# All products of a batch in halves of the rows, as one chain over three banks, from batch 1 on

## The reference

```python
def _attention(x, W_q, W_k, W_v, W_o):          # 16 heads of 16
    q, k, v = split(x @ W_q.T), split(x @ W_k.T), split(x @ W_v.T)
    attn = softmax(scale * einsum('bnqd,bnkd->bnqk', q, k))
    return merge(einsum('bnqk,bnkd->bnqd', attn, v)) @ W_o.T
...
x = x + a_alpha * _attention(_ada_rmsnorm(x, t, attn_gamma_w, attn_beta_w), W_q, W_k, W_v, W_o)
return x + f_alpha * _swiglu(_ada_rmsnorm(x, t, ffn_gamma_w, ffn_beta_w), gate_w, hidden_w, out_w, out_b)
```

## Time and profile before

| | us |
|---|---|
| median of 3 runs (lowest, highest) | 959.82 (959.23, 963.19) |
| the profiled execution, its own time | 960.88 |
| its span | 959.1 |

### The profile page before, as it was taken

One profiled execution on the slowest core, in us unless ns is written; L12 is line 12 of the kernel. 1 busy time (PEld: TensorE's weight loads), 2 busy tenths in 40 slices (PEclk: granted clock), 3 DMA queues, 4 the chain that ended last, 5 costly groups with the idle time before them and its releaser, 6 DMA issues.

```text
span 959.1 us, 18261 instructions
## 1 busy us (share of the span) xinstructions
PE 934.6 (97%) x6636; PEld 655.1 (68%) x6636; DVE 733.1 (76%) x1428; ACT 559.2 (58%) x1162; POOL 276.3 (29%) x262
## 2 busy tenths in 40 slices
PE   5999999999899999999999999999999999999998
PEld 4777777777544567767766766776677677666587
DVE  4787878999878788678778867886886788678253
ACT  5466555544566666476657646664765656476532
POOL 1256423222101033222313222231232223125142
PEclk9899999999999999999999999999999999999999
DMA  9646458434521213033022302312130222110000
GB/s 266 150 127 149 105 133 184 103 102 109 131 75 57 67 56 73 24 117 78 3 89 58 73 13 90 95 24 87 59 73 2 90 66 42 60 64 8 1 28 23
DMA packets 93754, 75.61 MB, mean 79 GB/s; under 512 B 44881, under 2 KB 79769, under 8 KB 93665
## 3 DMA queue, kind: packets, MB, share of 16 engines
q1 hardware_dynamic: 81880, 61.91, 24.5%
q10 hardware_dynamic: 11784, 12.54, 5.1%
HBM read 27.73 MB, written 12.61 MB: 42 GB/s over the span
## 4 chain that ended last, share of the span: by engine, by line
PE 86%; DVE 5%; ACT 3%; issue 2%; SPq 2%; DMA 1%; POOL 0%; ACTq 0%; DVEq 0%; POOLq 0%
PE bank L423 14%; PE bank L1083 13%; PE bank L1324 13%; PE bank L1064 9%; PE bank L1407 9%; PE raw_pair L998 5%; PE bank L1334 5%; PE bank L881 4%; PE bank L940 3%; PE bank L1146 2%; PE bank L1350 2%; PE bank L333 2%; DVE amax L486 2%; PE bank L1562 1%; PE bank L341 1%
## 5 line engine op out<-in xcount | busy, mean ns | idle before, releaser
L1072 ACT ACTIVATE probs<-bank 128x512 f32<-128x512 f32 x512 | 289.1, 599 | 201.7 <-PE bank L1064 200.5
L1008 DVE TENSOR_REDUCE rowmax<-raw_pair 128x1 f32<-128x512 f32 x488 | 325.6, 685 | 85.6 <-PE raw_pair L998 83.7
L423 PE MATMUL bank<-up_w,xs_part 128*128 128x512 f32 x768 | 193.9, 406 | 5.7 <-POOL xs_part L405 5.3
L1064 PE MATMUL bank<-q_stack,k_stack 50*128 50x512 f32 x480 | 185.9, 417 | 3.2 <-DMA q_stack<-shift_rows 1.4
L998 PE MATMUL raw_pair<-k_stack,q_stack 48*128 48x512 f32 x456 | 177.1, 413 | 0.0
L423 PEld LDWEIGHTS bank<-up_w,xs_part 128*128 128x128 f32 x768 | 144.2, 193 | 40.3 <-POOL xs_part L405 6.1
L1380 POOL TENSOR_TENSOR hid<-scratch,hid 128x512 fp32r<-128x512 f32 x64 | 84.3, 1317 | 206.1 <-ACT hid L1376 206.1
L1083 PE MATMUL bank<-probs,v_ext 128*17 128x512 f32 x1024 | 134.7, 598 | 0.6
L1064 PEld LDWEIGHTS bank<-q_stack,k_stack 50*128 50x128 f32 x480 | 82.8, 184 | 39.0 <-ACT probs L1072 25.5
L1407 PEld LDWEIGHTS bank<-out_w,hid 64*128 64x128 f32 x1152 | 87.2, 185 | 28.7 <-issue 20.4
L1407 PE MATMUL bank<-out_w,hid 64*128 64x256 f32 x1152 | 100.9, 288 | 0.2
(11 more groups left out here) (207 smaller groups left out, 1613.1 us busy)
## 6 DMA issues: line engine op xcount, KB each, us to landing
q_stack<-split SPq DMA_DIRECT2D x48, 128.0 KB, 3.4
q_stack<-hid SPq DMA_DIRECT2D x42, 128.0 KB, 2.9
k_stack<-hid SPq DMA_DIRECT2D x42, 128.0 KB, 2.9
xk<-xT SPq DMA_DIRECT2D x32, 128.0 KB, 3.0
xt<-x_tok SPq DMA_DIRECT2D x32, 128.0 KB, 2.8
x_spill<-x1t ACTq DMA_DIRECT2D x32, 128.0 KB, 2.5
xa_spill<-xa ACTq DMA_DIRECT2D x32, 128.0 KB, 2.4
x_in<-xa_spill SPq DMA_DIRECT2D x8, 512.0 KB, 5.1
```

Source lines behind the costliest of these rows:

```text
L423: last = nc.tensor.matmul(bank[j][:], xs_part[a][:, m % 2, k, :], up_w[w][:, k, col + j * W:col + (j + 1) * W], start=(i == 0), stop=(i == ...
L1008: nc.vector.reduce_max(rowmax[:, e + RAWS * half:e + RAWS * half + 1], raw_pair[:, half, :], AX.X) \
L1064: nc.tensor.matmul(score_bank[c % 2][:], k_rows[rows, slot, kt * P:(kt + 1) * P], q_rows[rows, slot, :], start=True, stop=True).then_inc(s ...
L1072: nc.scalar.activation(probs[:, (kt % 2) * J + j, :], score_bank[c % 2][:], ACT.Exp).then_inc(exp_done, 1)
```

## The change

- `plan` now gives every product of batches 1 to 7 to one chain: qk(1,0), qk(1,1) in half-step 0, then v(0), wo(0), wo(1), v(1), qk(0,0), qk(0,1) in half-steps 1 to 6, the transposes in 7, and from 8 on gate, hidden and out as before. Each is cut in lower and upper rows; the lower half of one runs beside the upper half of the one before, also across the end of a batch (the last out piece's upper half runs beside qk(1,0)'s lower half in half-step 0 of the next batch).
- The three banks of `turn_bank` are taken in turn by all products (`place`, `chain_bank`); v has counters of its own, `v_full` and `v_free`.
- Every product is complete half a step to a step later, and the consumers move: `head_act` and `head_dve` write out half-steps 0 to 7 for ScalarE and VectorE. The values of half-steps 2, 4, 6 move to the ends of 3, 4 and 6. wo waits for the high parts first and for the low ones at its eleventh matmul.
- Half-step 5 has no raw pair, 7 has two (`raws_of`). Before, that was so for no batch but the last, which left out one in 5 and ran one behind.
- The last two additions to the output of batch b - 1 move from the end of its batch into half-step 0 of the next (`out_dve`, `out_pool`), and its stores into `second_stacks_sp`, which issues ten of the twelve stack DMAs as their parts are ready; ScalarE issues the other two in half-step 3.
- In batch 7, which has no following batch, qk(0) is missing; v(1)'s upper half runs alone in half-step 5.

```diff
-        turn_bank = (psum[2], psum[3], psum[4])
+        turn_bank = (psum[3], psum[4], psum[2])
...
+        def raws_of(b, h, ffn):
+            if not ffn:
+                return [raw_at(b, h + AHEAD_FIRST)] if h < HALVES - (AHEAD_FIRST - AHEAD) else []
+            if h < RAW_PAUSE or h > RAW_PAUSE + 2:
+                numbers = [h + AHEAD]
+            else:
+                numbers = ([], [RAW_PAUSE + AHEAD], [RAW_PAUSE + AHEAD + 1, RAW_PAUSE + AHEAD + 2])[h - RAW_PAUSE]
+            return [raw_at(b, n) for n in numbers if b < B - 1 or n < RAWS * G]
...
+        def place(p):
+            if p[0] in ("gate", "hidden"):
+                return 8 + 2 * p[1] + (p[0] == "hidden")
+            if p[0] == "out":
+                return 8 + 2 * NH + p[1] // HALF
+            return {("qk", 1, 0): 0, ("qk", 1, 1): 1, ("v", 0): 2, ("wo", 0): 3, ("wo", 1): 4, ("v", 1): 5,
+                    ("qk", 0, 0): 6, ("qk", 0, 1): 7, ("xf", 1): 8, ("xf", 0): 9}[p]
+        PLACES = 8 + 2 * NH + 2
+        def chain_bank(b, p):
+            return turn_bank[(PLACES * (b - 1) + place(p)) % 3]
...
+        def chain_free_pe(pe, b, p, u, at):
+            def freed(w, count):
+                pe.wait_ge(pair_free[w], credited(pair_free[w], u + count))
+            hidden = at["hidden"]
+            if p[0] == "gate":
+                f = p[1]
+                freed(1, at["xf"][1] + 1 if f == 0 else hidden + max(f - 1, 0))
+            elif p[0] == "hidden":
+                freed(0, hidden + p[1])
+            elif p == ("out", 0, 0):
+                freed(1, hidden + NH - 1)
+            elif p == ("out", HALF, 0):
+                freed(0, hidden + NH)
+            elif p == ("qk", 1, 0):
+                freed(*((0, 0) if b == 1 else (1, -1)))
+            elif p == ("qk", 1, 1):
+                freed(1 if b == 1 else 0, 0)
+            elif p == ("v", 0):
+                freed(1, 0)
+            elif p == ("v", 1):
+                pe.wait_ge(v_free, 2 * (b - 1) + 1)
+            elif p[0] == "wo":
+                freed(p[1], at["qk1"][p[1]] + 1)
+            elif p[0] == "qk":
+                freed(p[2], at["wo"][p[2]] + 1)
...
+        def chain_lower_pe(pe, b, p, u, at):
+            c = b - 1
+            chain_free_pe(pe, b, p, u, at)
+            if p == ("gate", 0):
                 pe.wait_ge(f_in_high, c + 1)
                 pe.wait_ge(f_in_copied, c + 1)
+            elif p[0] == "qk":
+                pe.wait_ge(q_in_low, credited(q_in_low, (b if p[1] == 1 else b + 1) + 1))
+            elif p == ("wo", 0):
+                pe.wait_ge(on_high, c * GP + GP)
+            elif p[0] == "out":
+                n = OUT_PIECES.index(p[1:])
+                if n >= 2:
+                    pe.wait_ge(upper_done, (len(OUT_PIECES) - 2) * c + n - 1)
+                pe.wait_ge(prod_low, credited(prod_low, c * NH + NH // 2 * (p[2] + 1)))
...
+            steps = chain_steps(p)
+            each = len(steps) // 6
+            for i, step in enumerate(steps):
+                if p == ("gate", 0) and step[0] == 1:
+                    pe.wait_ge(f_in_low, credited(f_in_low, KD * c + (2 - step[2])))
+                elif p == ("wo", 0) and i == 10:
+                    pe.wait_ge(on_low, credited(on_low, c * GP + GP))
+                last = chain_matmul(b, p, i, step, LOWER, len(steps))
+                if i == len(steps) - 1:
                     last.then_inc(lower_done, 1)
-                yield
...
+        def chain_upper_pe(pe, b, p, u, at, lowers):
             pe.wait_ge(lower_done, lowers)
+            if p[0] == "qk":
+                w = p[2]
+                pe.wait_ge(pair_free[w], credited(pair_free[w], u + at[f"qk{p[1]}"][w]))
+            elif p[0] == "wo":
+                pe.wait_ge(pair_free[p[1]], credited(pair_free[p[1]], u + at["wo"][p[1]]))
+            elif p[0] == "v":
+                pe.wait_ge(v_free, 2 * (b - 1) + p[1])
+            elif p[0] == "out" and p[1] % HALF == HALF - 1 and p[2] == 1:
+                m = p[1] // HALF
+                pe.wait_ge(pair_free[m], credited(pair_free[m], u + at["out"]))
...
-        XF_AT, FFN_AT, OUT_AT, SPLIT_NEXT = 6, 8, 24, 25
+        XF_AT, FFN_AT, OUT_AT, SPLIT_NEXT = 7, 8, 24, 25
...
+            table[1:5] = [("v", 0)], [("wo", 0)], [("wo", 1)], [("v", 1)]
             if following:
+                table[5:7] = [("qk", 0, 0)], [("qk", 0, 1)]
...
+        VALUES_LATE = {3: 0, 4: 1, 6: 2}
+        def chain_batch_pe(pe, b, u, following, pending):
+            table, at = plan(True, following), uses(True, following)[0]
+            lowers = LOWERS * (b - 1)
+            def chain(p, middle=None):
+                nonlocal pending, lowers
+                beside_pe(None if p is None else chain_lower_pe(pe, b, p, u, at), pending, middle)
+                lowers += p is not None
+                pending = None if p is None else chain_upper_pe(pe, b, p, u, at, lowers)
+            for h in range(HALVES):
+                n = h // 2
+                def values():
+                    pb, pg = last_of(b, n // T) if n % T == 0 else (b, n // T)
+                    values_pe(pe, pb, pg, (n - 1) % T)
+                def second():
+                    excursion_pe(pe, b, h, True, (1,))
+                    if h % 2 == 0 and h > FFN_AT:
+                        values()
+                excursion_pe(pe, b, h, True, (0,))
+                if h == 0:
+                    values()
+                    chain(table[h][0])
+                    second()
+                    chain(table[h][1])
+                elif h < XF_AT:
+                    if table[h] or pending is not None:
+                        chain(table[h][0] if table[h] else None, second)
+                    else:
+                        second()
+                    if h in VALUES_LATE:
+                        kt = VALUES_LATE[h]
+                        if kt % HALF == 0:
+                            pe.wait_ge(v_free, 2 * (b - 1) + kt // HALF + 1)
+                        values_pe(pe, b, 0, kt)
+                    if not following and h in LAST_FILLS:
+                        fill_last_pe(pe, h, u, at)
+                elif h == XF_AT:
+                    second()
+                    xf_pe(pe, b - 1, both(u, at["xf"]))
+                    if not following:
+                        fill_behind_pe(pe, u, at)
+                elif h == FFN_AT:
+                    second()
+                    values()
+                    chain(table[h][0])
+                elif following or h < OUT_AT:
+                    chain(table[h][0], second)
...
+        def head_act(act, b, h, u, at, following):
+            if h == 1:
+                qk_act(act, 1, 0, u + at["qk1"][0], chain_bank(b, ("qk", 1, 0)))
+                exp_act(act, b, 0, 0, 2)
+                normalise_act(act, b - 1, GP - 1)
+                exp_act(act, b, 0, 0, 3)
+                return
+            if h == 2:
+                qk_act(act, 1, 1, u + at["qk1"][1], chain_bank(b, ("qk", 1, 1)))
+            elif h == 3:
+                chain_v_act(act, b, 0)
+            elif h == 6:
+                chain_v_act(act, b, 1)
+            elif h == XF_AT and following:
+                qk_act(act, 0, 0, u + at["qk0"][0], chain_bank(b, ("qk", 0, 0)))
+            exps_act(act, b, h)
+            if h == 3:
+                act.wait_ge(pair_free[1], credited(pair_free[1], u + at["qk1"][1] + 1))
+                for half in range(2):
+                    stack_dma(act, b, 1, 1, half, 1)
+            elif h in (4, 5):
+                squares_act(act, b - 1, h - 4)
+            elif h == 6:
+                normed_act(act, b - 1)
+            elif h == XF_AT:
+                xf_act(act, b - 1, both(u, at["xf"]), b + 2 if following else b + 1)
...
+                if following and h == FFN_AT + 1:
+                    qk_act(act, 0, 1, u + at["qk0"][1], chain_bank(b, ("qk", 0, 1)))
...
+        def head_dve(dve, b, h, u, at, before, following):
+            first, second = functools.partial(maxima_dve, dve, b, h, True, 1), functools.partial(maxima_dve, dve, b, h, True, 0)
+            if h == 0:
+                if before is not None:
+                    out_dve(dve, b - 2, 0, before)
+                first()
+                sums_dve(dve, b - 1, G - 1)
+                divide_dve(dve, b - 1, G - 1)
+                if before is not None:
+                    out_dve(dve, b - 2, 1, before)
+                second()
+                turn_dve(dve, b - 1, GP - 1)
+            elif h == 1:
+                first()
+                qk_dve(dve, 1, 0, 4 * b + 2, chain_bank(b, ("qk", 1, 0)))
+                second()
+            elif h == 2:
+                qk_dve(dve, 1, 1, 4 * b + 2, chain_bank(b, ("qk", 1, 1)))
+                first()
+                second()
+            elif h == 3:
+                first()
+                second()
+            elif h in (4, 5):
+                m = h - 4
+                wo_dve(dve, b - 1, m, u + at["wo"][m])
```

(47 more changed lines are left out.)

521 lines of the change are left out of this document (243 added, 278 removed).

## The result

| | before | after |
|---|---|---|
| median of 11 runs each, same chip (us) | 959.16 | 968.25 |
| the profiled execution, its own time | 960.88 | 970.81 |
| its span | 959.1 | 969.0 |
| ratio of the times, 95% interval | | 1.0103 [1.0087, 1.0119] |

The account below looks back on a forecast made before the run. TensorE, busy 97% of the span, was taken as the bound: its instruction stream plus its waits. Batches summed as 5 x 0.65 + 2.0 + 0.5 = 5.8 us, added to 959.82 for 965.6 us; range 957 to 971.

Parts of the forecast that it names:

- The lone halves and the work of the chain: Half-steps 0 to 8: pairing lone halves saves 1.5 us a batch; TensorE's own work becomes 25.26 us, 2.55 less.
- the 0.20 of half-step 3: Half-step 3's first raw half waits 0.2 us, since maxima queue behind the copies of q and k.
- rival B: Mixed groups cost 0.235 and half-step 7's wait is 0.6 shorter: 960.4 us, no difference; chance 0.22.
- scores alone, which still take a slot each: Half-step 5, without a raw pair: scores were taken to need their own slots, giving 2.08 us.
- Half-step 7's wait: The second raw pair waits for VectorE's maxima, queued behind a subtraction waiting for ScalarE's copy: 2.24 us.
- Half-step 8's wait: The gate's sixth lower waits 0.76 us for GpSimd's second low part, with qk(0,1)'s product now in the chain.
- Rival D: The granted clock falls behind half-step 7's idle stretch, adding 5 to 9 us: 971 to 975; chance 0.08.
- in the batches before it stays at 1.00: Argument against a clock fall: the granted clock stayed at 1.00 in the batches of the kernel before.
- Stack transfers, costed at nothing: Stack DMAs end by 12.3 us plus some 3 for landing; half-step 6's raw half needs them at 17.4.
- TensorE does the same work in both: Outside half-steps 0 to 8 nothing changes, so the stretch's difference is that of the batch.
- A: Half-step 7's second raw pair is hidden in time TensorE stands still anyway: 951 us; chance 0.12.
- C: Groups mixing 512- and 256-column halves cost 0.34 us: +10 us, about 970 if half comes true; chance 0.10.

Follow-up runs that it names:

- edits 3 and 4: Two runs, each against the kernel before: the changed kernel with ScalarE's qk(0,0) copy before the normalised rows, 954.94 us; with half-step 7's first maxima before VectorE's subtraction, 954.6 us.
- experiment 1: The changed kernel with five unused 512-column matmuls in half-step 7 before the second raw pair: 961.4 us, ratio 1.0036 to the kernel before.
- experiment 3: The changed kernel with ScalarE copying qk(0,0) at the end of half-step 6, ahead of the normalised rows: 954.94 us, ratio 0.9965 to the kernel before.
- experiment 5: The changed kernel with one raw pair in each of half-steps 5, 6 and 7, the chain kept: 964.28 us, ratio 1.0062 to the kernel before.
- experiment 4: The changed kernel with VectorE taking half-step 7's first two maxima ahead of the qk(0,0) subtraction: 954.6 us, ratio 0.9969 to the kernel before.
- the old order: The kernel before, products untouched, with no raw pair in half-step 5 and two in 7 in batches 1 to 6: 977.46 us, ratio 1.0196.
- experiment 7: The kernel before with no raw pair in half-step 5, two in 7, and four unused matmuls in that wait: 967.0 us, ratio 1.0107.

## Why the prediction came out as it did

The median lies 2.65 above the forecast and inside the range, and a part of that is luck: 10.4 us that the forecast lacked (the clock, the stacks, half-steps 7 and 8) and 6.6 us that it had too much cancel in part.

- **The lone halves and the work of the chain: right, and cheaper than I took them.** Half-steps 0 to 6 were forecast at 20.35 with the 0.20 of half-step 3; they took 19.63 (batches 1 and 2). I had 0.25 for a 512-column half beside two of 256, and it is 0.235, as rival B had it: in batch 3's half-step 0 the groups start at 490.58, 490.81, 491.05 and so on:

```profile
490.81 0.39 PE L1378 MATMUL bank<-xf_part,wq 64*128 64x512 f32 x1
490.82 0.40 PE L1392 MATMUL bank<-out_w,hid 64*128 64x256 f32 x2
491.05 0.39 PE L1378 MATMUL bank<-xf_part,wq 64*128 64x512 f32 x1
```

  Half-step 5 was forecast at 2.08, "scores alone, which still take a slot each", and took 1.71 to 1.74. A lone score runs beside a lone half of the product, in the other half of the array, and needs no slot of its own: that sentence of the prediction was wrong. In batch 3's half-step 5 they start together, and the next half follows 0.22 later:

```profile
504.55 0.39 PE L1378 MATMUL bank<-xa_part,wq 64*128 64x512 f32 x1
504.56 0.39 PE L1076 MATMUL bank<-q_stack,k_stack 50*128 50x512 f32 x1
```

  In sum 0.72 a batch, 4.3 us for six.
- **Half-step 7's wait: right in mechanism and size.** Forecast 4.18 us for the half-step, measured 4.25 in batch 1, and 4.24 with fillers. Every link is in the rows: subtraction 0.61 behind the copy, maxima behind that, bank free 0.73 after the maximum began. The Trainium skill (TensorEngine Tiling, PSUM Bottleneck) says that tiling speeds up TensorE and not the emptying of PSUM, and advises both ScalarE and VectorE for it; the trace agrees, with TensorE standing 1.47 us for a bank that VectorE has to read. Both engines are used here, and the order in their queues decides: edits 3 and 4 take 0.9 us off by order alone.
- **Half-step 8's wait: right (0.63 for 0.76),** but seen only where the clock stays up.
- **The clock: the step that failed.** Rival D had a chance of 0.08, with "in the batches before it stays at 1.00" against it. That says little: before, batches 1 to 6 have no recorded wait over 0.11 us, and the longest of batch 7 is this one:

```profile
851.44 0.49 PE L1064 MATMUL bank<-q_stack,k_stack 50*128 50x512 f32 x1 [0.78 <-ACT probs L1072]
```

  The one row that spoke on the matter, had the clock fall behind 1.91 us of waiting, and my own sum put 2.24 us of waiting into every batch. The fall came in all seven, and cost 8.2 us (6.9 and 1.3, experiment 1), at the upper end of D's 5 to 9. Forecast and rival D were not two cases: the wait that the forecast put in is the one behind which the clock fell. That it falls behind every such wait doesn't follow, though (experiments 3 and 5), so D was likely, not certain.
- **Stack transfers, costed at nothing: wrong by 1.1 us in the profiled execution.** I had them end by 12.3 + 3 against a need at 17.4. In batch 6 they hold half-step 6 by 0.6 us, in batch 4 by 0.4, in the others by 0.1 or less (by the half-step's length over 3.02; the list of waits has only batch 6's, as 0.2, since it counts from the end of the last matmul). The issues end later than I had them: at 12.4 us behind half-step 0 in batch 2, near the forecast, but at 13.1 to 14.0 in the other five, and landing took 3.3 more in experiment 5. SP works through them back to back, most in 0.60 us each, but in each of these five batches one issue takes 1.1 to 2.2 us. In batch 3 it is among the last four (the third of them takes 1.63):

```profile
498.72 3.54 SPq L914 DMA_DIRECT2D k_stack<-hid  x4
```

  Such an issue is in the kernel before too (1.55 us in batch 3); what makes it long isn't shown.
- **Outside the stretch: "TensorE does the same work in both" holds for batches 1 to 6** (57.53 for 57.63 us), but not for batch 7. There the kernel before had this, from half-step 9 to 24's first score (TensorE's waits):

```profile
PE bank L1064 <- DMA q_stack<-shift_rows: 1.4, 2, 0.7
```

  and its 38.78 us became 36.51 with no wait. The two waits stand before the first scores of half-steps 16 and 24, which need a group's shift; these half-steps came 0.95 and 0.92 us later than their like. Before, the last batch left out one raw in half-step 5 and ran one behind, so its shifts came late; after, all batches have the same positions. That gave 2.3 us I had not counted, 1.9 of it by these two waits; the other 0.4 lies in half-steps 21 to 23, and half-step 24, 2.43 us long for 1.99, gives as much back.
- **Rivals A and C.** A (the second pair hidden, 951) didn't happen because of VectorE's order, as its "against" said, and experiments 3 and 4 show that even without the subtraction 0.6 us of the wait stays. C (a mixed group dearer) is excluded by the 0.235.

The account on the profiled executions: forecast +5.8; -4.3 half-steps 0 to 6; +1.1 half-steps 7 and 8 (8.30 for 8.11, six times); +8.2 clock; +1.1 stacks; -2.3 batch 7 from half-step 9 on. That is +9.6, of the +9.9 between the spans. Left out are phase 1 (+0.4), the rest of batches 1 to 6 (-0.6 in sum) and batch 7 from half-step 24 on (+0.5).

## What to carry to other kernels

When a forecast puts a new wait in front of TensorE, price in the same breath what the clock may do behind it; if nothing useful can fill the wait, matmuls that do nothing can. When a stage uses the same double buffer twice, the second use waits for everything that stands ahead of the consumer's read in its queue, so look at that order and not only at how long the read takes: one raw pair in another half-step turned +1% into -1.4%. And a move that relieves one place (here the stacks' late landing in half-step 5) should be checked at the place it moves to.

## What the runs showed of the hardware

- The granted clock fell to 0.50 or 0.51 in every batch behind a recorded wait of 1.26 to 1.48 us and, in the old order, behind one of only 0.76 to 0.83 us; with matmuls in these waits (experiments 1 and 7) it fell in none. The low stretches were 3.4 us long, or twice that. The wait's length alone doesn't decide. The clock stayed at 1.00 behind 0.57 to 0.59 us (experiments 3 and 4, batches 1 to 6), behind 0.78 us in batch 7 of the kernel before and behind 2.00 us in batch 5 of experiment 5; and in batch 7, behind the same 1.25 us, it stayed up in experiment 3 and fell in experiment 4. I can't say from these runs what decides. The Trainium skill (TensorE: Matmul & The Clock Gate, A second HAM failure mode: psum-queue depth-cycling) tells of another kernel in which frequent short pauses from cycling through PSUM banks made the clock swing. Here too the pause is one for a bank, but it was one recorded pause a batch; whether it is the same case isn't shown.
- A matmul of 512 columns on one half of the rows beside two of 256 on the other costs 0.235 us, the same as two of 512.
- SP issues a stack transfer in 0.60 us, one behind the other, but in five of the batches 1 to 6 one of the row took 1.1 to 2.2 us. In the kernel before, where ScalarE issues none of them, it was 1.55 to 1.60 us in three of the six.
